# Attention with a mixture of experts on one core: routing in smaller pieces at two places of VectorE's step, the store of each slot tile right behind its copy, 79 slot tiles in place of 80

## The chip, the cores and the metric

One core of a Trainium2 chip runs the whole program. The metric is the device time of one execution in microseconds; less is better.

## The reference, cut to what matters

The input x has 16 sequences of 512 tokens with 256 features. Both branches read the same normalised rows.

```python
xn = layernorm(x)
# attention: 16 heads of 64, causal
q, k, v = xn @ Wq[h], xn @ Wk[h], xn @ Wv[h]
att = concat_h(softmax(causal(q @ k.T / 8)) @ v) @ Wo + bo
# mixture: 16 experts of width 128, the best two for each token
score = sigmoid(xn @ gate_w + gate_b)
value, index = top_k(score, 2);  value /= value.sum()
mlp(x, g, u, d) = (silu(x @ g) * (x @ u)) @ d
moe = xn + mlp(xn, shared) + sum_n value[n] * mlp(xn, expert[index[n]])
out = x + att + moe
```

## The kernel before, in words

**Stage A** (`stage_a`, about the first 100 us) normalises all rows, stores them to DRAM (`xn_rows`), splits the attention weights into a high and a low part for matmuls of three passes, and computes the gate scores.

**Stage D** (`stream`) runs over 128 units u, eight for each sequence; a unit is two heads of one sequence. One unit is a software pipeline: TensorE transposes the normalised probabilities of unit u (L685), computes the scores of unit u + 1 (L696), projects keys, values and queries of unit u + 2 (L658, L671), applies the output projection to a unit two back (L726), and at the end weighs the values of unit u (L710). VectorE takes the row maxima out of the score banks, splits keys and queries (L990) and attention outputs (L1001, the first instruction of its next step) and adds the output projection into `base` (L1015). ScalarE takes the exponentials (L853) and makes the high parts. GpSimd divides the probabilities (L1289) and issues the indirect DMAs. SyncE issues all other DMAs; its loop has four slots in each unit, and `pace` (L493) holds each slot until TensorE has come to a place of the unit: slot 0 waits for the first transposes, slot 1 for the last ones, slot 2 for the projected keys, slot 3 for the projected queries.

All TensorE results go through eight PSUM banks in ring order. `order` (L453) lists the bank users of a unit, and `emptied` (L464) says which semaphore frees a bank; TensorE waits for it before it writes. In a unit with slot tiles the last banks are taken by `dn`, `gu`, `xt` (a slot tile's output, its gate and up projection, its transposed rows) and `w`. So the first score banks of the next unit are the ones that the copy of `dn` (ScalarE, `take_y`, L893), the gate product of `gu` (VectorE, L1135 and L1140) and the split of `xt` (VectorE, `split_xt`, L1145) have to free, and the last of these four is freed by L1001. In a plain unit L1001 frees the same bank.

**The experts.** In units 0 to 9 VectorE runs one piece of `route(u)` (L1048) at the very end of each step: best two experts of each token, token counts by matmul with a matrix of ones (`count`, L757, at `SUMS_AT` and `RANKS_AT`), 16 prefix scans (L1075, L1078), a slot number for each token and expert, and the expert of each slot tile. The helper `then` puts a semaphore wait behind each routing instruction. Each expert's tokens fill whole slot tiles of 256 rows. From unit `FIRST_SCATTER` = 10 on, 32 units scatter the rows to their slots in DRAM (`queued_rows`), and every second unit from 12 on (`PACK_AT`) splits the weights of an expert on ScalarE and VectorE and stores them. `clear` (L513) has zeroed the slots before.

From `FIRST_TICK` = 46 on each unit has two ticks, part 0 after the scores and part 1 before L710. Tick n transposes tile n (L794), expands tile n - 1 (L784) and brings down tile n - 2 (L771). ScalarE copies the result of tile n - 2 into the one buffer `y` (L897), behind a wait for the store of the tile before it (`y_stored`). SyncE loads the rows two ticks ahead (L547) and stores `y` (`store_y`, L550). In the kernel before it stores tile n - 3 at tick n, in slot 1 for part 0 and slot 3 for part 1. GpSimd gathers each tile's weights (L1264).

After the last tick, from unit 88 on, `ITEMS` (L421) gives two blocks of 128 tokens to each unit: GpSimd gathers their two expert rows and VectorE adds them one unit later (`add_routed`, L1166). The last two sequences have their blocks in fixed units, 110 to 113 and 118 to 121, so that units 110 to 113 have three blocks each.

Of the kernel before, what the change touches and what calls it, by code (L numbers as in the profile page):

```python
# [25 lines left out]
ALU = mybir.AluOpType  # L26
# [3 lines left out]
P = 128  # L30
# [5 lines left out]
NTOK = B * T  # L36
# [9 lines left out]
SLOT_TILES = 2 * NTOK // SLOT_TILE + E  # L46
# [8 lines left out]
FIRST_SCATTER = 10  # L55
# [247 lines left out]
def stream(nc, ins, dram, keep, out):  # L303

    with ExitStack() as ctx:
# [65 lines left out]
        made, routing, both_ready, route_step = sem("made"), sem("routing"), sem("both_ready"), sem("route_step")  # L371
# [118 lines left out]
        with nc.Block() as block:  # L490
            @block.sync
            def _(sp):
# [96 lines left out]
                for u in STEPS:  # L589
                    b, k = u // PAIRS, u % PAIRS  # L590
                    for slot in range(4):
                        pace(u, slot)

                        if 0 <= u < ZERO_PARTS // 8:
                            for n in range(2):
                                clear(u * 8 + slot * 2 + n)
# [29 lines left out]
                        if n is not None and slot % 2:  # L626
# [341 lines left out]
            def _(dve):  # L968
# [79 lines left out]
                def route(u):  # L1048

                    if u == 0:  # L1050
# [4 lines left out]
                        mark_highest(0)  # L1055
                    elif u == 1:
                        choose(0)
                        then(dve.scalar_tensor_tensor(flat(gates), flat(chosen[0]), -4.0, flat(gates), ALU.mult, ALU.add))
                        then(dve.tensor_reduce(best[1][:, :], gates[:, :, :], AX.X, ALU.max))
                    elif u == 2:  # L1060
                        mark_ties(1)
                        choose(1)
                    elif u == 3:
# [5 lines left out]
                    elif u == SUMS_AT:  # L1069
# [4 lines left out]
                        for e in range(6):  # L1074
                            then(dve.tensor_tensor_scan(spots[:, :, e], ones[:, :], tile_sum[:, :, e], 0.0, ALU.mult, ALU.add))  # L1075
# [303 lines left out]
```

## Time and profile before

| what | value |
|---|---|
| median of 3 runs (lowest to highest) | 2058.46 us (2057.05 to 2064.8) |
| the profiled execution | 2058.73 us, its span 2057.0 us |
| mean granted TensorE clock over the span | 0.967 |
| TensorE busy | 1957.2 us, 95% |
| VectorE busy | 1406.4 us, 68% |
| ScalarE busy | 1204.1 us, 59% |
| GpSimd busy | 1015.5 us, 49% |
| chain that ended last | TensorE 70%, GpSimd 11%, issue 9% |

The busy share of TensorE is high, but a matmul that runs at half clock is busy too. So it is to be read together with the granted clock, and by stretches of the span and not over the whole. The span includes everything from the first instruction to the last; the execution's own time is 1.7 us above it.

### The profile page before, as it was taken

To read this page: it belongs to the slowest core of one execution; us is meant where nothing else is said; L and a number is where in the kernel's file an instruction comes from. 1 tells how busy PE (TensorE), PEld (TensorE's weight loads), DVE (VectorE), ACT (ScalarE), POOL (GpSimd) and SP (SyncE) were. 2 spreads that over 40 slices of the span, in tenths; PEclk is the share of its full clock that TensorE was granted. 3 is DMA by queue.
4 is the path that set the end of the run, shared out by engine and by line. 5 is a ranking of instruction groups with operands and counts; after the bars stand their busy time and mean duration, and the time that the engine had idled before them with its cause. 6 is when DMAs were issued, how large, how long until landed. Compare 5 with 4: busy or idle time off the path is not lost.

```text
span 2057.0 us, 53505 instructions
## 1 busy us (share of the span) xinstructions
PE 1957.2 (95%) x20580; PEld 1788.7 (87%) x20580; DVE 1406.4 (68%) x4090; ACT 1204.1 (59%) x3344; POOL 1015.5 (49%) x1513
## 2 busy tenths in 40 slices
PE   6889999999999999999999999999999999999998
PEld 6868888888898888898888898898898989888997
DVE  7567776767676756566566566566567888887775
ACT  4355556666665655556565565555566666655664
POOL 2232447777776543333333333343336777776552
PEclk9998999999999999999999999999999999998999
DMA  9524333434343224544544544444422232323100
GB/s 262 178 93 159 140 126 100 147 106 143 110 144 103 88 94 129 175 133 135 166 128 149 165 136 140 158 133 145 157 95 86 85 115 86 116 85 93 48 28 12
DMA packets 159435, 251.50 MB, mean 122 GB/s; under 512 B 27344, under 2 KB 113104, under 8 KB 159184
## 3 DMA queue, kind: packets, MB, share of 16 engines
q1 hardware_dynamic: 135376, 151.58, 22.8%
q0 software_dynamic: 23808, 96.49, 14.7%
q8 instruction: 167, 2.74, 0.6%
q14 instruction: 84, 0.69, 0.1%
HBM read 152.59 MB, written 95.42 MB: 121 GB/s over the span
## 4 chain that ended last, share of the span: by engine, by line
PE 70%; POOL 11%; issue 9%; DMA 2%; ACT 2%; DVE 1%; SPq 0%; POOLq 0%; ACTq 0%; DVEq 0%
PE d_bank L658 14%; PE d_bank L696 11%; PE d_bank L710 10%; PE d_bank L685 9%; PE d_bank L671 7%; POOL d_probs L1289 7%; PE d_bank L726 6%; PE d_bank L784 6%; POOL queued_rows L1252 4%; PE d_bank L771 3%; DMA routed_rows<-d_y 2%; PE d_bank L742 2%; PE d_bank L794 1%; ACT d_probs L853 1%; PE d_bank L731 1%
## 5 line engine op out<-in xcount | busy, mean ns | idle before, releaser
L1289 POOL TENSOR_SCALAR d_probs<-d_probs,d_inverse 128x512 f32<-128x512 f32 (+3 forms) x1024 | 550.6, 551 | 858.8 <-DVE d_inverse L985 857.1
L853 ACT ACTIVATE d_probs<-d_probs,d_bias 128x512 f32<-128x512 f32 (+3 forms) x1024 | 561.1, 553 | 1.2 <-DVE d_bias L979 1.2
L979 DVE CUSTOM_DVE_ANT_0 d_probs<-d_bank,mask 128x512 f32<-128x512 f32 (+3 forms) x1024 | 439.9, 484 | 5.1 <-PE d_bank L696 5.0
L658 PE MATMUL d_bank<-d_xnt,wqk_all 128*128 128x512 f32 x1536 | 422.7, 412 | 1.5 <-DVE d_xnt L1032 1.5
L696 PE MATMUL d_bank<-d_ks,d_qs 64*128 64x512 f32 (+3 forms) x3072 | 339.4, 348 | 53.7 <-issue 51.8
L696 PEld LDWEIGHTS d_bank<-d_ks,d_qs 64*128 64x128 f32 x3072 | 264.3, 197 | 85.3 <-issue 71.2
L658 PEld LDWEIGHTS d_bank<-d_xnt,wqk_all 128*128 128x128 f32 x1536 | 279.4, 194 | 56.7 <-DVE d_xnt L1032 1.7
L846 ACT ACTIVATE d_probs_t<-d_bank 128x512 f32<-128x512 f32 (+1 forms) x384 | 188.0, 525 | 234.0 <-PE d_bank L685 233.7
L710 PE MATMUL d_bank<-d_probs_t,d_v 128*64 128x128 f32 x5120 | 309.2, 276 | 0.0
L710 PEld LDWEIGHTS d_bank<-d_probs_t,d_v 128*64 128x64 f32 x5120 | 278.3, 137 | 17.1 <-issue 5.4
L685 PEld LDWEIGHTS d_bank<-ident_r,d_probs_moved 64*128 64x128 f32 x5120 | 237.7, 137 | 40.8 <-issue 38.3
L685 PE MATMUL d_bank<-ident_r,d_probs_moved 64*128 64x64 f32 x5120 | 260.6, 247 | 9.4 <-POOL d_probs L1289 9.3
L990 DVE TENSOR_TENSOR d_qs<-d_bank,d_qs 128x512 fp32r<-128x512 f32 x128 | 88.5, 692 | 199.6 <-ACT d_qs L859 199.6
L972 DVE COPY d_probs_t<-d_bank 128x512 f32<-128x512 f32 (+1 forms) x384 | 217.4, 594 | 4.6 <-PE d_bank L685 4.2
L671 PEld LDWEIGHTS d_bank<-wv_all,d_xnt 128*128 128x128 f32 x1536 | 202.9, 193 | 11.9
L726 PEld LDWEIGHTS d_bank<-wo_all,d_out_t 128*128 128x128 f32 x1536 | 200.1, 189 | 12.2 <-issue 1.7
L726 PE MATMUL d_bank<-wo_all,d_out_t 128*128 128x256 f32 x1536 | 205.8, 280 | 1.5 <-DVE d_out_t L1001 1.5
L871 ACT ACTIVATE d_out_t<-d_bank 128x512 fp32r<-128x512 f32 x128 | 76.0, 593 | 218.8 <-PE d_bank L710 215.8
L671 PE MATMUL d_bank<-wv_all,d_xnt 128*128 128x256 f32 x1536 | 203.6, 283 | 0.0
L853 ACT ACTIVATION_READ_ACCUMULATOR d_probs<-d_probs,d_bias 128x1 f32 x1024 | 196.2, 192 | 0.0
L1135 DVE SCALAR_TENSOR_TENSOR d_slot_hid<-d_slot_hid,d_bank 128x256 f32<-128x256 f32 x80 | 33.7, 421 | 211.8 <-ACT d_slot_hid L904 211.8
L897 ACT ACTIVATE d_y<-d_bank 128x512 f32<-128x512 f32 x80 | 47.8, 597 | 209.9 <-DMA routed_rows<-d_y 209.9
(124 smaller groups left out, 2473.5 us busy)
## 6 DMA issues: line engine op xcount, KB each, us to landing
queued_rows<-d_zeros SPq DMA_DIRECT2D x80, 256.0 KB, 2.4
d_x<-queued_rows SPq DMA_DIRECT2D x80, 256.0 KB, 3.1
routed_rows<-d_y SPq DMA_DIRECT2D x80, 256.0 KB, 3.8
expert_rows<-d_w SPq DMA_DIRECT2D x32, 384.0 KB, 3.0
a_x_in<-in_L_attn_x SPq DMA_DIRECT2D x16, 512.0 KB, 7.0
xn_rows<-a_xn SPq DMA_DIRECT2D x16, 512.0 KB, 5.2
d_normal<-xn_rows SPq DMA_DIRECT2D x32, 256.0 KB, 3.4
d_base<-in_L_attn_x SPq DMA_DIRECT2D x32, 256.0 KB, 3.1
```

The costliest lines, as they stand in the source:

```text
L658: last = pe.matmul(to[:, :], wqk[:, n % PAIRS, "qk".index(kind), wa, k, :], xnt[n // PAIRS % 2][:, xb, k, :], start=first, stop=(k == KD - ...
L671: last = pe.matmul(to[:, t * 2 * P:(t + 1) * 2 * P], xnt[b % 2][:, xa, k, tok * P:(tok + 1) * P], wv[:, wb, k, cols], start=(k == 0 and (x ...
L685: last = pe.transpose(to[r][:, off:off + DK].bitcast(F32R), moved[half(r), i, h, j * P:(j + 1) * P], ident[half(r), half(r)])
L696: last = pe.matmul(to[h][:, at * P:at * P + cols], qs[r][qa][half(h), i * P:(i + 1) * P], ks[r][kb][half(h), 0:cols], start=(n == 0), stop ...
L710: last = pe.matmul(to[half(h), i * P:(i + 1) * P], v[u // 2 % 2][:, j, col:col + DK], probs_t[fill][:, h, at + j, :], start=(j == 0), stop ...
L726: last = pe.matmul(to[:, s * D:(s + 1) * D], out_t[g % 2][oa][:, j, cols], wo[:, wb, g % 4 * GROUP + j, :], start=(j == 0 and n == 0), sto ...
L784: last = pe.matmul(to[:, part * SLOT_TILE:(part + 1) * SLOT_TILE], w[t % 3][:, wa, cols(k)], xt[:, xb, k, :], start=(n == 1), stop=(n == K ...
L846: act.activation(probs_t[fill][:, :, :, half(0)], bank(f"t{fill}", u)[:, 0:2 * slots * DK].rearrange("p (h j n) -> p h j n", h=2, n=DK), A ...
L853: act.activation(part, part, ACT.Exp, bias=bias[:, i, h:h + 1], scale=-1.0, accum_out=total[which][:, at % 4:at % 4 + 1]).then_inc(exp_don ...
L972: dve.tensor_copy(probs_t[fill][:, :, :, half(1)], bank(f"t{fill}", u, 1)[:, 0:2 * slots * DK].rearrange("p (h j n) -> p h j n", h=2, n=DK ...
L979: dve.tensor_tensor_reduce(out=probs[:, i, h, 0:cols], in0=bank(f"s{fill}", u, h)[:, at * P:at * P + cols], in1=mask[:, T - cols:T], scale ...
L1289: pool.tensor_scalar(part, part, inverse[which][:, at % 4:at % 4 + 1], 1.0, ALU.mult, ALU.mult).then_inc(norm_done, 1)
```

## The change

It has three parts. (1) `route` takes a second argument. Its early half runs after the maxima and the first `invert` of the step, ahead of the split of the keys; its late half runs where the whole piece ran. The work of units 0 to 9 is spread over units 0 to 12; the count matmuls move from units 4 and 6 to 5 and 8. `FIRST_SCATTER` goes from 10 to 12, the packs from even units from 12 on to odd units from 15 on, `FIRST_TICK` from 46 to 49. (2) `store_y(n - 2)` is issued in slot 2 of the unit for a tick of part 0, and in slot 0 of the next unit for a tick of part 1. (3) `SLOT_TILES` is 79 and not 80, and so is the number of `clear` transfers. The last tick is then part 0 of unit 89, the blocks of `ITEMS` begin in unit 91 and not in 88, and unit 118 has three of them too.

```diff
-SLOT_TILES = 2 * NTOK // SLOT_TILE + E
+SLOT_TILES = (2 * NTOK + E * (SLOT_TILE - 1)) // SLOT_TILE
-FIRST_SCATTER = 10
+FIRST_SCATTER = 12
...
-        PACK_AT = {FIRST_SCATTER + 2 + 2 * e: e for e in range(E)}
-        SUMS_AT, RANKS_AT = 4, 6
+        PACK_AT = {FIRST_SCATTER + 3 + 2 * e: e for e in range(E)}
+        SUMS_AT, RANKS_AT = 5, 8
-        FIRST_TICK = FIRST_SCATTER + 2 * B + 4
+        FIRST_TICK = FIRST_SCATTER + 2 * B + 5
...
-                        sp.wait_ge(routing, 9)
+                        sp.wait_ge(slots_known, 1)
...
-                        sp.wait_ge(routing, 10)
+                        sp.wait_ge(experts_known, 1)
...
-                            if 3 <= n:
-                                store_y(n - 3)
-                        if u == LAST_TICK + 1 and slot == 0:
-                            store_y(SLOT_TILES - 1)
+                        n = TICKS.get((u, 0)) if slot == 2 else TICKS.get((u - 1, 1)) if slot == 0 else None
+                        if n is not None and n >= 2:
+                            store_y(n - 2)
...
+                def mark_ties(n):
+                    then(dve.tensor_tensor(work[:, :, :], gates[:, :, :], by_e(best[n]), ALU.is_equal))
+                def rank_ties():
+                    then(dve.tensor_tensor(work[:, :, :], work[:, :, :], rank_of_e[:, None, :].broadcast_to([P, TT, E]),
+                                           ALU.mult))
+                def choose(n):
+                    then(dve.tensor_reduce(mark[:, :], work[:, :, :], AX.X, ALU.max))
+                    then(dve.tensor_tensor(chosen[n][:, :, :], work[:, :, :], by_e(mark), ALU.is_equal))
+                def scan(experts):
+                    for e in experts:
+                        then(dve.tensor_tensor_scan(spots[:, :, e], ones[:, :], tile_sum[:, :, e], 0.0, ALU.mult, ALU.add))
+                def spot_of(n):
+                    then(dve.tensor_tensor(work[:, :, :], chosen[n][:, :, :], spots[:, :, :], ALU.mult))
+                def slot_of(n):
+                    then(dve.tensor_reduce(mark[:, :], work[:, :, :], AX.X, ALU.add))
+                    then(dve.tensor_copy(keep["slot"][n][:, :], mark[:, :]))
+                def route(u, late):
+                    if (u, late) == (0, 0):
                         dve.wait_ge(made, 8)
                         then(dve.tensor_copy(rank_of_e[:, :], small["rank_i"][:, :]))
                         then(dve.tensor_copy(tile_start[:, :], tile_i[:, :]))
                         then(dve.tensor_copy(small["row"][:, 0:1], small["row_i"][:, 0:1]))
+                    elif (u, late) in ((0, 1), (2, 1)):
+                        n = u // 2
+                        then(dve.tensor_reduce(best[n][:, :], gates[:, :, :], AX.X, ALU.max))
+                        mark_ties(n)
+                    elif (u, late) in ((1, 0), (3, 0)):
+                        rank_ties()
+                    elif (u, late) in ((1, 1), (3, 1)):
+                        choose(u // 2)
+                    elif (u, late) == (2, 0):
                         then(dve.scalar_tensor_tensor(flat(gates), flat(chosen[0]), -4.0, flat(gates), ALU.mult, ALU.add))
+                    elif (u, late) == (4, 0):
                         then(dve.tensor_tensor(sum_best[:, :], best[0][:, :], best[1][:, :], ALU.add))
                         then(dve.reciprocal(sum_best[:, :], sum_best[:, :]))
                         for n in range(2):
                             then(dve.tensor_tensor(keep["weight"][n][:, :], best[n][:, :], sum_best[:, :], ALU.mult))
+                    elif (u, late) == (4, 1):
                         dve.tensor_tensor(both[:, :, :], chosen[0][:, :, :], chosen[1][:, :, :], ALU.add).then_inc(both_ready, 1)
+                    elif (u, late) == (SUMS_AT, 1):
                         dve.wait_ge(sums_ready, 1)
                         for n in range(2):
                             dve.tensor_copy(flat(tile_sum)[:, n * T:(n + 1) * T], bank(f"sum{n}", u)[:, :]).then_inc(sums_out, 1)
                         dve.wait_ge(sums_out, 2)
+                        scan(range(3))
+                    elif (u, late) == (6, 0):
+                        scan(range(3, 7))
+                    elif (u, late) == (6, 1):
+                        scan(range(7, E))
+                    elif (u, late) == (7, 0):
                         then(dve.tensor_scalar(padded[:, :], spots[:, TT - 1, :], float(SLOT_TILE - 1), None, ALU.add))
                         then(dve.tensor_copy(padded_i[:, :], padded[:, :]))
                         shift = SLOT_TILE.bit_length() - 1
...
                         then(dve.tensor_copy(padded[:, :], padded_i[:, :]))
                         then(dve.tensor_tensor_scan(ends[:, :], ones[:, 0:E], padded[:, :], 0.0, ALU.mult, ALU.add))
                         then(dve.tensor_tensor(offset[:, :], ends[:, :], padded[:, :], ALU.subtract))
+                    elif (u, late) == (7, 1):
                         then(dve.tensor_tensor(spots[:, :, :], spots[:, :, :], tile_sum[:, :, :], ALU.subtract))
                         then(dve.tensor_tensor(spots[:, :, :], spots[:, :, :], offset[:, None, :].broadcast_to([P, TT, E]),
                                                ALU.add))
+                    elif (u, late) == (RANKS_AT, 1):
                         dve.wait_ge(ranks_ready, 1)
                         for n in range(2):
                             part = flat(spots)[:, n * T:(n + 1) * T]
                             dve.tensor_tensor(part, bank(f"rank{n}", u)[:, :], part, ALU.add).then_inc(ranks_out, 1)
                         dve.wait_ge(ranks_out, 2)
+                    elif (u, late) in ((9, 0), (10, 0)):
+                        spot_of(u - 9)
+                    elif (u, late) in ((9, 1), (10, 1)):
+                        slot_of(u - 9)
+                        if u == 10:
+                            dve.sem_inc(slots_known, 1)
+                    elif (u, late) == (11, 1):
                         then(dve.tensor_tensor(past[:, :, :], tile_start[:, :, None].broadcast_to([P, SLOT_TILES, E]),
                                                ends[:, None, :].broadcast_to([P, SLOT_TILES, E]), ALU.is_ge))
+                    elif (u, late) == (12, 0):
                         then(dve.tensor_reduce(expert[:, :], past[:, :, :], AX.X, ALU.add))
+                    elif (u, late) == (12, 1):
                         then(dve.tensor_scalar(expert[:, :], expert[:, :], float(E - 1), float(P), ALU.min, ALU.mult))
                         then(dve.tensor_scalar(expert[:, :], expert[:, :], small["row"][:, 0:1], None, ALU.add))
                         then(dve.tensor_copy(keep["weight_row"][:, :], expert[:, :]))
+                        dve.sem_inc(experts_known, 1)
...
                         invert(31, u + 1)
+                    route(u, 0)
...
-                    if 0 <= u < 10:
-                        route(u)
+                    route(u, 1)
```

`mark_ties` is one comparison, `rank_ties` one multiplication, `choose` a reduction and a comparison, `spot_of` one multiplication, `slot_of` a reduction and a small copy; `scan` is one prefix scan for each expert.

## Rows read from the trace of the kernel before

**Rows 1.** By stretch: length, busy PE, PEld, DVE, ACT, POOL, then clock, DMA share, GB/s.

```profile
128.00:302.00 174.00, 157.67 (x1586) 138.44 (x1586) 130.98 (x346) 89.67 (x255) 66.32 (x107) 0.89 0.40 138
...
738.00:1529.00 791.00, 757.27 (x7664) 701.11 (x7660) 489.71 (x1390) 461.59 (x1263) 283.55 (x448) 0.95 0.45 143
1529.00:1832.00 303.00, 302.48 (x3454) 273.52 (x3452) 242.17 (x714) 190.25 (x553) 213.86 (x304) 1.00 0.31 95
1832.00:1894.00 62.00, 58.52 (x590) 51.09 (x589) 47.50 (x130) 32.73 (x94) 47.57 (x63) 0.89 0.32 95
```

**Rows 2.** Waits of the slot stage, 738 to 1529 us: total us, times, longest.

```profile
ACT d_y L897 <- DMA routed_rows<-d_y: 209.9, 78, 7.6
...
PE d_bank L696 <- issue: 31.2, 32, 3.7
```

**Rows 3.** Timeline around one stall: start us, us, engine, line, what, idle before it.

```profile
974.73 1.63 PE L658 MATMUL d_bank<-d_xnt,wqk_all 128*128 128x512 f32 x6
...
977.26 1.08 POOL L1264 DMA_INDIRECT d_w<-expert_rows,weight_row  x1 [0.17 <-issue]
...
980.42 0.87 PE L771 MATMUL d_bank<-d_w,d_slot_hs 128*128 128x256 f32 x6
...
980.69 0.71 SPq L552 DMA_DIRECT2D routed_rows<-d_y  x1
...
987.85 0.60 ACT L897 ACTIVATE d_y<-d_bank 128x512 f32<-128x512 f32 x1 [7.32 <-DMA routed_rows<-d_y]
...
989.55 0.68 DVE L1145 TENSOR_TENSOR d_xt<-d_bank,d_xt 128x512 fp32r<-128x512 f32 x1
...
989.74 2.67 PE L696 MATMUL d_bank<-d_ks,d_qs 64*128 64x512 f32 x12 [3.28 <-issue]
```

**Rows 4.** Stores of y, line L552, from issue to landing.

```profile
DMA to landing us min/median/max: 2.1/3.8/7.6
```

**Rows 5.** As rows 1: eight plain units, one slot unit, a gap and what followed.

```profile
379.40:481.20 101.80, 100.46 (x1156) 91.36 (x1154) 71.72 (x213) 66.40 (x188) 72.86 (x105) 1.00 0.38 126
...
1010.70:1028.30 17.60, 17.60 (x192) 16.61 (x192) 9.56 (x31) 10.60 (x30) 6.27 (x10) 1.00 0.45 144
...
1102.80:1106.20 3.40, 2.07 (x32) 1.57 (x31) 2.57 (x6) 2.88 (x7) 0.00 (x0) 1.00 0.55 221
1106.20:1124.40 18.20, 18.20 (x168) 16.68 (x168) 12.38 (x34) 10.62 (x29) 7.72 (x12) 1.00 0.40 120
```

**Rows 6.** Chain of waits, 1062 to 1084 us: start us, us, what.

```profile
1065.36 0.64 issue
...
1066.95 0.71 issue
...
1072.84 2.22 PE d_bank L784 x12
...
1081.74 1.44 PE d_bank L784 x12
```

**Rows 7.** Timeline of TensorE at the first slot tile.

```profile
743.51 0.72 PE L794 MATMUL d_bank<-ident_r,d_x 128*128 128x128 f32 x4 [2.45 <-DVE d_bias L979]
```

**Rows 8.** Timeline of VectorE and TensorE in unit 2 and behind it.

```profile
163.06 0.69 DVE L990 TENSOR_TENSOR d_qs<-d_bank,d_qs 128x512 fp32r<-128x512 f32 x1 [2.34 <-ACT d_qs L859]
...
164.53 1.22 DVE L1116 TENSOR_TENSOR d_work<-gates,d_best 128x1024 f32<-128x1024 f32 x1
...
169.85 0.69 DVE L1001 TENSOR_TENSOR d_out_t<-d_bank,d_out_t 128x512 fp32r<-128x512 f32 x1
...
170.64 1.01 PE L696 MATMUL d_bank<-d_ks,d_qs 64*128 64x256 f32 x6 [2.60 <-issue]
```

**Rows 9.** The same in unit 9 and behind it.

```profile
271.95 1.49 DVE L1102 TENSOR_TENSOR d_past<-d_tile_start,d_ends 128x1280 f32<-128x1280 f32 x1
...
276.67 1.01 PE L696 MATMUL d_bank<-d_ks,d_qs 64*128 64x256 f32 x6 [2.52 <-issue]
```

**Rows 10.** Timeline of VectorE, unit 4: six scans.

```profile
197.51 1.93 DVE L1075 TENSOR_TENSOR_SCAN d_spots<-d_ones,d_tile_sum 128x64 f32<-128x64 f32 x6
```

More of the change, by code:

```diff
@@ L370, in stream @@
         zeroed, zero_stored = sem("zeroed"), sem("zero_stored")
-        made, routing, both_ready, route_step = sem("made"), sem("routing"), sem("both_ready"), sem("route_step")
+        made, both_ready, route_step = sem("made"), sem("both_ready"), sem("route_step")
+        slots_known, experts_known = sem("slots_known"), sem("experts_known")
         sums_ready, sums_out, ranks_ready, ranks_out = sem("sums_ready"), sem("sums_out"), sem("ranks_ready"), sem("ranks_out")
@@ L592, in _ @@
                         pace(u, slot)
-                        if 0 <= u < ZERO_PARTS // 8:
-                            for n in range(2):
-                                clear(u * 8 + slot * 2 + n)
+                        for n in range(u * 8 + slot * 2, u * 8 + slot * 2 + 2):
+                            if 0 <= n < ZERO_PARTS:
+                                clear(n)
                         if u in (FIRST_SCATTER - 1, FIRST_SCATTER):
@@ L1073, in route @@
                         dve.wait_ge(sums_out, 2)
-                        for e in range(6):
-                            then(dve.tensor_tensor_scan(spots[:, :, e], ones[:, :], tile_sum[:, :, e], 0.0, ALU.mult, ALU.add))
-                    elif u == 5:
-                        for e in range(6, E):
-                            then(dve.tensor_tensor_scan(spots[:, :, e], ones[:, :], tile_sum[:, :, e], 0.0, ALU.mult, ALU.add))
+                        scan(range(3))
[4 more added lines that the diff above has]
+                    elif (u, late) == (7, 0):
                         then(dve.tensor_scalar(padded[:, :], spots[:, TT - 1, :], float(SLOT_TILE - 1), None, ALU.add))
@@ L1086, in route @@
                         then(dve.tensor_tensor(offset[:, :], ends[:, :], padded[:, :], ALU.subtract))
-                    elif u == RANKS_AT:
+                    elif (u, late) == (7, 1):
                         then(dve.tensor_tensor(spots[:, :, :], spots[:, :, :], tile_sum[:, :, :], ALU.subtract))
@@ L1095, in route @@
                         dve.wait_ge(ranks_out, 2)
-                    elif u in (7, 8):
-                        n = u - 7
-                        then(dve.tensor_tensor(work[:, :, :], chosen[n][:, :, :], spots[:, :, :], ALU.mult))
-                        then(dve.tensor_reduce(mark[:, :], work[:, :, :], AX.X, ALU.add))
-                        then(dve.tensor_copy(keep["slot"][n][:, :], mark[:, :]))
-                    elif u == 9:
+                    elif (u, late) in ((9, 0), (10, 0)):
[5 more added lines that the diff above has]
+                    elif (u, late) == (11, 1):
                         then(dve.tensor_tensor(past[:, :, :], tile_start[:, :, None].broadcast_to([P, SLOT_TILES, E]),
                                                ends[:, None, :].broadcast_to([P, SLOT_TILES, E]), ALU.is_ge))
+                    elif (u, late) == (12, 0):
                         then(dve.tensor_reduce(expert[:, :], past[:, :, :], AX.X, ALU.add))
+                    elif (u, late) == (12, 1):
                         then(dve.tensor_scalar(expert[:, :], expert[:, :], float(E - 1), float(P), ALU.min, ALU.mult))
@@ L1107, in route @@
                         then(dve.tensor_copy(keep["weight_row"][:, :], expert[:, :]))
-                    dve.sem_inc(routing, 1)
-                def mark_highest(n):
-                    then(dve.tensor_reduce(best[n][:, :], gates[:, :, :], AX.X, ALU.max))
-                    mark_ties(n)
-                def mark_ties(n):
-                    then(dve.tensor_tensor(work[:, :, :], gates[:, :, :], by_e(best[n]), ALU.is_equal))
-                    then(dve.tensor_tensor(work[:, :, :], work[:, :, :], rank_of_e[:, None, :].broadcast_to([P, TT, E]),
-                                           ALU.mult))
-                def choose(n):
-                    then(dve.tensor_reduce(mark[:, :], work[:, :, :], AX.X, ALU.max))
-                    then(dve.tensor_tensor(chosen[n][:, :, :], work[:, :, :], by_e(mark), ALU.is_equal))
+                        dve.sem_inc(experts_known, 1)
                 def split_hidden(u):
```

11 lines of the change are left out of this document (removed).

## The prediction

> **What bounds the kernel now.** I read the windows by stretch first, then the waits of the worst stretch, then its timeline. In the windows the reader compares three columns: the length, the busy time of TensorE, and its granted clock. In the plain units from 1529 to 1832 us TensorE is idle for 0.5 of 303 us at clock 1.00: these are at their floor. In the slot stage, 738 to 1529 us, it is idle for 791.0 - 757.3 = 33.7 us, and the clock of 0.95 costs 0.05 * 791 = 40 us more. The first units (128 to 302 us) have 16.3 us idle and 0.11 * 174 = 19 us of clock; 1832 to 1894 us has 3.5 and 0.11 * 62 = 7 us [rows 1]. TensorE bounds all of it, and what can be won is its idle time and the half clock behind it.
>
> In the slot stage ScalarE waits 209.9 us, 78 times, for the store of `y` to land, and TensorE 31.2 us in front of L696 for something the view can't name ("issue") [rows 2]. The timeline names it: a store is issued at 980.69, ScalarE's next copy starts only at 987.85 when it has landed, VectorE's split of `xt` follows at 989.55, and TensorE's scores stand 3.28 us until 989.74, because they write the banks that these instructions free [rows 3]. The copy had long been done when its store was issued, since the store has its place half a unit behind it; so landing times of 2.1, 3.8 (median) and 7.6 us [rows 4] fall just in front of the next copy.
>
> How the clock hangs on this: the two small gaps at 1065.36 and 1066.95 us are followed by expansions of 2.22 us in place of 1.44 [rows 6]: 1.2 instead of 2.4 GHz. After 1.3 us of gap at 1102.8 to 1106.2 the clock stayed 1.00 [rows 5]. So a gap makes a fall likely, not certain; where there is none (1529 to 1832 us) there is no fall.
>
> **Part 2, the store.** For a tick of part 0 the store is now issued once the keys are projected. In the unit of rows 3 L658 ends at 974.73 + 1.63 = 976.4, and ScalarE makes that tick's copy ahead of its split of those keys: the store starts some 4 us earlier than 980.69, and is ahead of the weight gather at 977.26. With 3.8 us it lands at 980.2, before the next result is due (980.42 + 0.87 = 981.3); with 7.6 us at 984.0. TensorE stands only if the copy comes later than about 984.5: the copy at 987.85 cost 3.28 us. For part 1 it is issued behind the first transposes of the next unit; the next copy is due some 5 to 7 us behind them (in the unit of rows 6 the expansion L784 that follows its matmuls starts at 1072.84, 7.5 us behind the transposes). There 3.8 us fit, and 7.6 us make a wait of up to 2 us on ScalarE with no TensorE work soon behind it. So nearly all of the idle time goes. What stays is the start: the first tile's rows are loaded in the very unit that transposes them, 2.45 us [rows 7], plus a fall, together some 4 us; and I leave 3 us for the units in which `base`, `normal` and `partial` are moved in slots 2 and 3 ahead of the store on SyncE. Gain 33.7 + 40 - 4 - 3 = 67; the undisturbed units say a little less: one takes 17.6 us against 101.8 / 8 = 12.7 in a plain one, 4.9 for two tiles [rows 5], which over 41 units (the first and last partly filled) leaves some 65 us of excess, 61 without the start. I take 60, after the 3 us. Bounds: 30 (the clock falls stay) and 70. The new wait on SyncE (for the copy) has in its queue behind it the loads of rows for the next tick, which are due half a unit later; it costs nothing unless a copy is over 4 us late. What is late next is nothing: ScalarE is busy 461.6 and VectorE 489.7 of 791 us [rows 1].
>
> **Part 1, the routing.** Today a piece ends the step and L1001 waits behind it. In unit 2 four instructions of 1.2 to 1.4 us run from 164.53 to 169.85, 5.3 us, and TensorE stands 2.60 us: some 2.7 us fit [rows 8]. In unit 9 the shared expert fills the end of the step; a piece of 3.9 us (271.95 to about 275.9) costs 2.52 us, so 1.4 fit [rows 9]. New late pieces: two instructions of 1.25, 2.5 us, in units 0 to 3; at most nine scans in unit 6, at 1.93 / 6 = 0.32 [rows 10] 2.9 us; two instructions of 2.7 in unit 7; 1.3 to 2.3 elsewhere. With 1.4 us of room in units 0 and 1 (1.1 us over in each), about 1.9 in unit 3 (0.6), 2.7 in units 6 and 7 (0.2 each) and 0.5 for units 8 to 12, the gaps sum to 3.7 in place of 16.3. The early pieces, 0.5 to 1.5 us, lie in the 2.34 us that VectorE waits for the queries [rows 8]; they delay the split of the keys, which no one needs before the next unit, so zero; if that cover were gone, 13 units by 1.2 would be 15 us. The clock: with three gaps of near 1 us I keep about 7 of 19 us. Gain 12.6 + 12 = 24 to 25; bounds 10 (cover half gone, falls stay) and 33. The packs move to odd units, where VectorE has 0.6 us more of its own and the same room as above for their one instruction; zero, bounds 0 and 6. Scatters, packs and ticks keep their spacing and only start later.
>
> **Part 3, one tile less.** A tile is 4.9 / 2 = 2.4 us of TensorE [rows 5]; one transfer of `clear` less is hidden behind other work.
>
> **The end.** A unit with three blocks costs: units 110 to 113 hold 10 us of idle time and clock in three stalled units [rows 1], 3.4 each. Unit 118 becomes another one, so plus 3. All others keep two blocks.
>
> Sum, against the profiled execution of 2058.7 (span 2057.0 and 1.7 around it), which stands within 0.3 of the median: 2058.7 - 60 - 24.5 - 2.4 + 3 = 1974.8. I say **1975**.
>
> **The clock rule.** By the trace, gaps as small as 0.64 and 0.71 us precede falls [rows 6]. The Trainium skill, page "TensorE: Matmul & The Clock Gate", section "HAM oscillation — how this bites in real kernels", tells of falls only after idle stretches longer than any gap but one or two here. If that were all, these falls would have another cause and would survive: only idle time would go. That is rival A.
>
> **Rivals.**
> A. The falls stay in the slot stage and in the routing units. Then 33.7 - 7 = 27, 12.6, 2.4 are won and 3 lost: 2020. For it: after like gaps the clock fell once and once it did not [rows 5, 6], so another cause may have its part. Against: none in 303 us of plain units, and fall follows gap in rows 6. Chance 0.12.
> B. Part of the stores still land late. SP reaches slot 2 behind up to three other transfers in two units of eight, and the store now runs beside the gather. If a third of the gaps and falls stay, 24 us less is won, with somewhat more left in the routing: 2000. Chance 0.22.
> C. The other side: the stores collide with the gathers of weights. At 45% DMA share [rows 1] a store takes the longest time seen, 7.6 us. Then part 1's copy slips 2 to 3 us into each unit, ScalarE passes that on to the query split, and TensorE stands perhaps 1.2 us and loses 1.7 by clock in each of 40 units: 116 us in place of 74 today, 42 more, against 24.5 + 2.4 - 3 won: 2077. It decides from a landing of over 6 us in most units. The Trainium skill, page "DMA: Bandwidth & Descriptors", section "Issuing engines are not separate DMA queues", says that transfers of SyncE and GpSimd share the same engines and interleave, which is this collision's ground. Against: the median is 3.8 with loads and gathers under way already. Chance 0.03.
> D. The stalls at L696 come from elsewhere and the store only shifts a wait: parts 1 and 3 alone, 2058.7 - 24.5 - 2.4 + 3 = 2035; if the routing then also gains nothing, 2058. Chance 0.06, of which 0.02 within 0.5% of today.
>
> **Numbers.** My forecast (1960 to 1990) has 0.57. The range holds forecast and B and most of the spread between: 1958 to 2008; A, C and D lie outside. A measurement of this kernel tells 0.5% (10 us) from no change. Faster by over that: 0.95; within: 0.02; slower: 0.03.
>
> **What would show it.** ScalarE's wait for the store falls from 209.9 us to under 40; the waits in front of L696 in the slot stage to under 6 us; the clock of that stretch at 0.99 or more; eight slot units take about 142 us. In units 1 to 13 the idle time is near 4 us and at most two falls remain; a gap of about 1.4 us appears behind unit 119. Wrong would be: a clock that stays near 0.95 without gaps (A), copies that still wait 3 us (B), landings of 6 us and more (C), or gaps of the same size with no ScalarE wait (D).

## The result and the profile after

| | before | after |
|---|---|---|
| median of the runs of the result | 2058.70 us (4 runs) | 1968.07 us (4 runs, 1964.47 to 1973.94) |
| profiled execution, its span | 2058.73 us, 2057.0 us | 1970.11 us, 1968.4 us |
| mean granted TensorE clock over the span | 0.967 | 0.989 |

The ratio is 0.9557, 95% interval 0.9525 to 0.9589: 91 us less, where 84 were forecast and 1958 to 2008 us was the range. The page of the profile after: busy time, the span in 40 slices, the granted clock in tenths.

```profile
PE 1905.5 (97%) x20558; PEld 1751.7 (89%) x20558; DVE 1406.9 (71%) x4086; ACT 1208.4 (61%) x3340; POOL 1019.5 (52%) x1512
...
PE   6889999999999998999999999999999999999998
...
PEclk9999999999999999999999999999999999999999
```

TensorE's busy time fell by 51.7 us with almost the same instructions. Only one tile of work (some 2.4 us) is saved. TensorE runs at half clock for 138 us before and for 47 us after, and half of that difference, 46 us, is busy time that went. Such a stretch at 1.2 GHz is called a fall from here on. The windows, by stretch (length; busy PE, PEld, DVE, ACT, POOL; clock, DMA share, GB/s), answer to [rows 1]. The bounds are, within 0.5 us, the ends of L710 in units 0, 16, 48, 89, 109 and 127; the last row is eight undisturbed units of the slot stage.

```profile
131.20:342.90 211.70, 207.33 (x2300) 185.22 (x2299) 172.54 (x473) 128.23 (x370) 103.62 (x161) 0.98 0.36 127
...
752.30:1478.00 725.70, 718.78 (x7654) 674.45 (x7650) 488.62 (x1390) 467.00 (x1261) 286.23 (x452) 0.99 0.48 155
1478.00:1730.00 252.00, 251.65 (x2892) 228.08 (x2890) 202.06 (x594) 158.73 (x461) 175.24 (x249) 1.00 0.31 96
1730.00:1960.00 230.00, 221.45 (x2500) 199.30 (x2498) 173.13 (x500) 134.95 (x391) 143.64 (x208) 0.97 0.22 66
863.20:1003.40 140.20, 140.20 (x1508) 131.86 (x1506) 95.87 (x273) 92.08 (x248) 56.34 (x88) 1.00 0.50 163
```

In the slot stage (752.3 to 1478.0 us) TensorE is idle for 6.9 us and the clock is 0.99; before it was 33.7 us and 0.95. Eight undisturbed units take 140.2 us at clock 1.00 and without a microsecond of idle time.

Read off both traces by the same ends of units, and the half clock added up in each stretch:

| stretch | before, us (at half clock) | after, us (at half clock) |
|---|---|---|
| to the end of unit 0 | 128.0 (0) | 130.9 (3.4) |
| units 1 to 16 | 236.2 (37.5) | 211.7 (10.2) |
| plain units to the first tick, and from the last tick to unit 109 (52 units) | 664.6 (3.4) | 661.3 (3.4) |
| slot stage, 41 units | 791.1 (78.5) | 725.8 (13.7) |
| units 110 to 127 | 228.3 (17.1) | 229.8 (13.7) |

The stage of 41 units now begins and ends with a unit that holds the shared expert, and before with a shorter kind; so it has 3.3 us of length from the plain stretches, and its own gain is 791.1 - 725.8 + 3.3 = 68.6 us. The waits of the stage (total us, times, longest) answer to [rows 2]:

```profile
ACT d_y L897 <- PE d_bank L771: 55.1, 34, 2.9
...
ACT d_y L897 <- DMA routed_rows<-d_y: 6.3, 4, 5.4
...
PE d_bank L794 <- DMA d_x<-queued_rows: 4.6, 1, 4.6
...
PE d_bank L696 <- issue: 1.8, 2, 1.1
```

ScalarE's wait for the store went from 209.9 us and 78 times to 6.3 us and 4 times. TensorE's waits in front of L696 went from 31.2 us to 1.8. One typical store, in the view of [rows 3]:

```profile
905.00 0.36 SPq L553 DMA_DIRECT2D routed_rows<-d_y  x1
...
907.46 1.09 POOL L1280 DMA_INDIRECT d_w<-expert_rows,weight_row  x1 [0.16 <-issue]
...
911.80 0.87 PE L771 MATMUL d_bank<-d_w,d_slot_hs 128*128 128x256 f32 x6
...
912.71 0.60 ACT L897 ACTIVATE d_y<-d_bank 128x512 f32<-128x512 f32 x1 [2.93 <-PE d_bank L771]
...
915.36 0.68 DVE L1161 TENSOR_TENSOR d_xt<-d_bank,d_xt 128x512 fp32r<-128x512 f32 x1
...
917.67 1.32 PE L696 MATMUL d_bank<-d_ks,d_qs 64*128 64x512 f32 x12
```

The store is issued at 905.00, ahead of the weight gather; ScalarE reaches the next copy, is held up only by TensorE's own result of 911.80 to 912.67, and starts it at 912.71. The split of `xt` (now L1161) is done 1.6 us before TensorE asks for its bank at 917.67, and the scores run without a gap. Stores also land sooner, against [rows 4]:

```profile
DMA to landing us min/median/max: 2.1/2.3/8.3
```

### The profile page after: what moved, and what is told of

Same layout as the page of the kernel before. It is cut to its first block, busy times and chain, and to the rows that moved or that the text cites. A ratio compares the mean times of both kernels' runs of the same rounds, so it can differ in the third digit from the quotient of the medians.

```text
span 1968.4 us, 53517 instructions
## 1 busy us (share of the span) xinstructions
PE 1905.5 (97%) x20558; PEld 1751.7 (89%) x20558; DVE 1406.9 (71%) x4086; ACT 1208.4 (61%) x3340; POOL 1019.5 (52%) x1512
## 4 chain that ended last, share of the span: by engine, by line
PE 73%; POOL 12%; issue 7%; ACT 2%; DVE 1%; DMA 0%; POOLq 0%; SPq 0%; DVEq 0%
PE d_bank L658 15%; PE d_bank L710 11%; PE d_bank L696 10%; PE d_bank L685 9%; PE d_bank L671 7%; POOL d_probs L1305 7%; PE d_bank L726 7%; PE d_bank L784 6%; POOL queued_rows L1268 4%; PE d_bank L771 3%; PE d_bank L742 2%; ACT d_probs L853 2%; PE d_bank L794 1%; PE d_bank L731 1%; POOL d_base L1257 1%
## 5 line engine op out<-in xcount | busy, mean ns | idle before, releaser
L658 PE MATMUL d_bank<-d_xnt,wqk_all 128*128 128x512 f32 x1536 | 417.6, 408 | 1.5 <-DVE d_xnt L1032 1.5
L696 PE MATMUL d_bank<-d_ks,d_qs 64*128 64x512 f32 (+3 forms) x3072 | 317.4, 335 | 14.0 <-issue 12.0
L710 PE MATMUL d_bank<-d_probs_t,d_v 128*64 128x128 f32 x5120 | 308.6, 276 | 0.0
L710 PEld LDWEIGHTS d_bank<-d_probs_t,d_v 128*64 128x64 f32 x5120 | 277.7, 137 | 17.2 <-issue 5.4
L696 PEld LDWEIGHTS d_bank<-d_ks,d_qs 64*128 64x128 f32 x3072 | 252.0, 188 | 35.6 <-issue 19.4
L685 PEld LDWEIGHTS d_bank<-ident_r,d_probs_moved 64*128 64x128 f32 x5120 | 232.8, 136 | 38.6 <-issue 36.9
L685 PE MATMUL d_bank<-ident_r,d_probs_moved 64*128 64x64 f32 x5120 | 256.2, 244 | 10.1 <-POOL d_probs L1305 10.0
L1001 DVE TENSOR_TENSOR d_out_t<-d_bank,d_out_t 128x512 fp32r<-128x512 f32 x128 | 88.3, 690 | 113.5 <-ACT d_out_t L871 112.8
L1296 POOL DMA_INDIRECT d_rows<-routed_rows,slot x128 | 132.0, 1031 | 35.5 <-issue 33.6
```

The lines of the kernel that those rows point to most:

```text
L658: last = pe.matmul(to[:, :], wqk[:, n % PAIRS, "qk".index(kind), wa, k, :], xnt[n // PAIRS % 2][:, xb, k, :], start=first, stop=(k == KD - ...
L685: last = pe.transpose(to[r][:, off:off + DK].bitcast(F32R), moved[half(r), i, h, j * P:(j + 1) * P], ident[half(r), half(r)])
L696: last = pe.matmul(to[h][:, at * P:at * P + cols], qs[r][qa][half(h), i * P:(i + 1) * P], ks[r][kb][half(h), 0:cols], start=(n == 0), stop ...
L710: last = pe.matmul(to[half(h), i * P:(i + 1) * P], v[u // 2 % 2][:, j, col:col + DK], probs_t[fill][:, h, at + j, :], start=(j == 0), stop ...
L1296: pool.indirect_dma_start(out=rows[m % 4 // 2][:, m % 2 * 2 + n, :], out_offset=None, in_=dram["routed"][:, :], in_offset=bass.IndirectOff ...
```

## The experiments

Two theories were put against each other first. The one of the prediction: the late store of `y` holds the PSUM banks that the next unit's scores need, and each such gap can bring TensorE down from 2.4 to 1.2 GHz for some microseconds. The rivals: the clock falls have another cause (A), or the stalls come from elsewhere (D). In each group of runs the kernel before ran on the same chip; it had medians of 2059.5, 2060.4 and 2057.8 us.

**The old places of the store.**

```diff
-                        n = TICKS.get((u, 0)) if slot == 2 else TICKS.get((u - 1, 1)) if slot == 0 else None
-                        if n is not None and n >= 2:
-                            store_y(n - 2)
+                            if 3 <= n:
+                                store_y(n - 3)
+                        if u == LAST_TICK + 1 and slot == 0:
+                            store_y(SLOT_TILES - 1)
```

> The changed kernel with the stores of y back at their old places (tick n stores tile n - 3, in slot 1 and slot 3, behind the load of the next rows); routing and 79 tiles stay as changed. My theory (the late store holds the banks that TensorE's scores need, and the clock falls follow those gaps): about 2035 us, the slot stage again with some 30 us of idle time and a clock near 0.95, ScalarE waiting some 200 us for the store. Rival (the routing's gain carries most): under 2000 us. Rival D (the stalls come from elsewhere): 1968 us as before.

Measured: 2042.32 us, ratio to before 0.9916 (0.9892 to 0.9939). ScalarE waits 196.8 us for the store again, and the window over the 41 units of the stage shows the old length and the old clock:

```profile
754.80:1545.90 791.10, 759.52 (x7654) 702.11 (x7652) 489.94 (x1390) 461.39 (x1261) 284.89 (x452) 0.95 0.44 142
```

The whole stage is back, 791.1 us, with nothing else undone. 74 us hang on these lines.

**The store alone**, in the kernel before.

```diff
-                            if 3 <= n:
-                                store_y(n - 3)
-                        if u == LAST_TICK + 1 and slot == 0:
-                            store_y(SLOT_TILES - 1)
+                        n = TICKS.get((u, 0)) if slot == 2 else TICKS.get((u - 1, 1)) if slot == 0 else None
+                        if n is not None and n >= 2:
+                            store_y(n - 2)
```

> The kernel before with only the new places of the stores of y (tile n - 2, slot 2 and slot 0 of the next unit); routing at one place, 80 tiles. My theory: 2058.7 - 66 = about 1993 us; the slot stage without gaps and at clock 0.99 or more, units 1 to 10 as before with 16 us of gaps and clock 0.89. If the parts overlap, this run and the one with the old store place would not add up: their gains would sum to clearly more or less than the 90 us of the whole.

Measured: 1986.90 us, ratio 0.9637 (0.9616 to 0.9658), 73 us less than before. The windows over the slot stage and over units 1 to 16:

```profile
742.10:1464.60 722.50, 718.79 (x7662) 675.16 (x7662) 487.47 (x1390) 468.20 (x1263) 285.59 (x450) 0.99 0.48 157
131.20:368.80 237.60, 220.78 (x2300) 196.35 (x2300) 173.15 (x475) 130.36 (x372) 109.78 (x169) 0.91 0.37 128
```

The stage takes 722.5 us with 80 tiles, and the first units stay as they were (237.6 us, clock 0.91). The gains add up within the noise: 73 us of the store here and 17 of the rest in the run with the old store make 90, and the whole is 91. So no overlap of the parts shows.

**Only one of the two places early.**

```diff
-                        n = TICKS.get((u, 0)) if slot == 2 else TICKS.get((u - 1, 1)) if slot == 0 else None
+                        n = TICKS.get((u, 0)) if slot == 2 else TICKS.get((u - 1, 1)) if slot == 1 else None
```

> The changed kernel, but only the stores of part-0 ticks are early (slot 2); those of part-1 ticks are issued in slot 1 of the next unit, behind the row loads. My theory: only the copy near the end of a unit stands in front of the next unit's scores, and it waits for the part-0 store; so this one loses almost nothing, 1968 to 1975 us, with ScalarE waiting about 1 us for the store at each part-0 copy. Rival (ScalarE's lost time itself is the cost, wherever it falls): 40 waits of 1 us and more, 1990 us or above.

Measured: 1967.54 us, ratio 0.9553 (0.9531 to 0.9574): nothing lost. ScalarE's wait in the slot stage is real all the same:

```profile
ACT d_y L897 <- DMA routed_rows<-d_y: 37.2, 38, 3.0
```

There is no wait in front of L696 among the waits of this stage. 37 us of ScalarE's time, 1.0 us for each copy that waits and 3.0 at the most, cost nothing.

```diff
-                        n = TICKS.get((u, 0)) if slot == 2 else TICKS.get((u - 1, 1)) if slot == 0 else None
+                        n = TICKS.get((u, 0)) if slot == 3 else TICKS.get((u - 1, 1)) if slot == 0 else None
```

> The changed kernel, but only the stores of part-1 ticks are early (slot 0 of the next unit); those of part-0 ticks are issued in slot 3, behind the row loads. My theory: this is where the whole cost lay, so 2020 to 2035 us, gaps in front of L696 in the slot stage and a clock near 0.95. Rival (both places share the cost): near 2000 us.

Measured: 2039.72 us, ratio 0.9929 (0.9897 to 0.9961), a little above what was expected. Of the stage's waits:

```profile
ACT d_y L897 <- DMA routed_rows<-d_y: 172.4, 39, 7.9
...
PE d_bank L696 <- issue: 31.1, 35, 3.6
```

Half as many copies wait as in the kernel before, yet the loss is the whole one. These copies, the last of each unit, wait for the part-0 store, and the banks that TensorE wants next stand behind them. They are also the ones with the long waits: 4.4 us each (172.4 / 39) against 1.0 us (37.2 / 38) at the other place, and at this place too some twenty waits, up to 4.6 us, have no gap behind them. No run has long waits at the other place; so whether such waits would cost something there was not tried. One slot of SyncE's loop for the part-0 store, which also puts it ahead of the load of rows, is worth over 70 us (2039.72 against 1967.54).

**79 tiles alone**, in the kernel before.

```diff
-SLOT_TILES = 2 * NTOK // SLOT_TILE + E
+SLOT_TILES = (2 * NTOK + E * (SLOT_TILE - 1)) // SLOT_TILE
...
-                        if 0 <= u < ZERO_PARTS // 8:
-                            for n in range(2):
-                                clear(u * 8 + slot * 2 + n)
+                        for n in range(u * 8 + slot * 2, u * 8 + slot * 2 + 2):
+                            if 0 <= n < ZERO_PARTS:
+                                clear(n)
```

> The kernel before with 79 slot tiles and 79 clears only. My theory: one tile is 2.4 us of TensorE plus its share of the stage's stalls, 1 us: 2055 us, not to be told from 2058.7. Rival (the last tile's end matters more, since the gathers of the end wait for it): 2050 us or below.

Measured: 2057.75 against 2060.41 us, ratio 0.9983 (0.9968 to 0.9999): 2.7 us, about what a tile was reckoned at (2.4), at the edge of what 10 and 13 runs can tell from nothing.

**Gaps made on purpose**, in plain units that had none in front of the scores.

```diff
                     route(u, 1)
+                    if u in range(18, 38, 2):
+                        for _ in range(3):
+                            then(dve.tensor_reduce(mark[:, :], wqk[:, 0, :, :, :, :].bitcast(F32).rearrange(
+                                "p w a k (c e) -> p (w a k c) e", e=E), AX.X, ALU.max))
```

> The changed kernel with three more reductions of 1.22 us each at the end of VectorE's step in ten plain units (18, 20 to 36), where the trace showed no gap in front of the scores and no fall of the clock. It adds only work whose result nobody reads. My theory (a gap in front of the scores makes the clock fall): a gap of 1.0 to 1.3 us behind each of the ten, 11 us in all, and several falls of the granted clock right behind them, each 1.7 to 3.4 us more: 20 to 35 us over the changed kernel. Rival A (the falls have another cause, tied to the slot tiles): the ten gaps, 11 us, and the clock of that stretch stays 1.00.

Measured: 1996.26 us in its one execution, 28 us over the changed kernel. The timeline behind unit 22, the third of the ten, and then windows up to that gap, right behind it, and over the stretch with the added reductions:

```profile
422.24 3.72 DVE L1249 TENSOR_REDUCE d_mark<-wqk_all 128x64 f32<-128x1024 f32 x3
...
426.00 0.69 DVE L1001 TENSOR_TENSOR d_out_t<-d_bank,d_out_t 128x512 fp32r<-128x512 f32 x1
...
426.79 0.62 PE L696 MATMUL d_bank<-d_ks,d_qs 64*128 64x256 f32 x6 [1.34 <-issue]
```

```profile
342.30:427.00 84.70, 80.49 (x927) 72.11 (x925) 66.39 (x172) 51.88 (x145) 57.87 (x83) 1.00 0.37 123
427.80:434.60 6.80, 6.80 (x38) 6.10 (x36) 4.57 (x19) 4.60 (x14) 3.65 (x6) 0.50 0.41 136
342.30:611.10 268.80, 256.63 (x2796) 229.27 (x2794) 206.84 (x539) 161.91 (x452) 180.48 (x254) 0.96 0.36 118
```

Three reductions keep L1001 until 426.00, TensorE stands 1.34 us, and 1 us later its clock is 0.50 for 6.8 us. All ten units show a gap, of 1.03 to 1.43 us, 12.8 us together; six of the ten are followed by a fall within 2.5 us. Units 17 to 48 hold 37.5 us at half clock in place of 3.4; 3.4 us of the growth belong to a fall that the changed kernel has too, behind a gap of 2 us in front of L685, and that lasts longer here. TensorE's idle time in these units grew from 6.1 to 16.2 us, since some shorter waits went. 10.1 + 34.1 / 2 = 27.2 us is the growth of that stretch (438.1 against 409.3 us, 28.8 us) to 2 us. No slot tile is at work in these units, and a gap alone brings falls: rival A's other cause isn't needed. The two gaps before this one (1.4 and 1.0 us) brought no fall, so a gap of this size makes one likely and not certain. All this rests on one execution.

**The second place of the routing taken away**, its spread over 13 units kept.

```diff
                         invert(31, u + 1)
-                    route(u, 0)
...
+                    route(u, 0)
                     route(u, 1)
```

> The changed kernel, but the early halves of the routing run at the end of the step too, directly ahead of the late halves; the spread over units 0 to 12 stays. My theory: some 13 us of early pieces come behind the late ones in units that have 1.4 to 2.7 us of room, so about 8 us of gaps more and 5 to 8 us of clock: 1980 to 1985 us, all of it in units 1 to 13. Rival (spreading over 13 units was the gain and the second place adds nothing): 1968 to 1970 us.

Measured: 1988.73 us, against 1962.27 for the change in the same group of runs; ratio to before 0.9640 (0.9602 to 0.9679). The window over units 1 to 16:

```profile
130.80:367.30 236.50, 223.52 (x2300) 198.87 (x2300) 171.74 (x473) 128.87 (x369) 98.18 (x162) 0.90 0.32 113
```

236.5 us: to 0.3 us the length in the kernel before. Seven gaps of 1.1 to 2.4 us, 11.8 us together, stand in place of four, and 47.8 us run at half clock in place of 10.2. I had expected 1980 to 1985 us, and it is more, because more falls followed. Against the kernel before, the spreading alone saved 4.7 us of idle time here and had 10.3 us more at half clock; the run with the store alone has the same ratio (0.9637). So the spreading alone shows no gain, and the routing's 24.5 us come with the place ahead of the key split (whether the place would do it without the spreading was not tried).

**The change again, in the last group.**

> The changed kernel once more, on the same chip as the three others: 1966 to 1970 us by any theory. It shows whether the late store of the first profile comes again: my theory says it is rare, so the slot stage without that gap, 719 to 721 us over 41 units.

Measured: 1962.27 us, ratio 0.9526 (0.9499 to 0.9553), a little below what I expected. Its slot stage takes 718.8 us; the late store of the first profile (told of below) is missing. But it isn't rare, as I had written: of the seven profiles with this order of the stores, that of this run alone is without the gap behind unit 66.

**Four mends of what was left.** Blocks of the end spread; first rows loaded a unit earlier; the store first in its slot; fewer scans in one piece.

```diff
-            for _ in range(2):
+            for _ in range(2 - sum(u == item[0] for item in ITEMS)):
                 if waiting and u >= waiting[0][0] * PAIRS + 12:
```

> The changed kernel, but a unit that holds a fixed block of the last two sequences takes only one waiting block, so that no unit has three. My theory: the five gaps of 0.6 to 2 us behind units 111 to 114 and 119, 6.5 us in all, go with their falls of the clock (10 us at half clock, 5 us): 1957 to 1960 us. Rival (the gaps come from the gathers' landing or from SyncE, not from VectorE's third block): no change, 1968 us.

Measured: 1955.23 us, ratio 0.9490 (0.9465 to 0.9515). The window from 1730 to 1850 us, in which the changed kernel had 5.0 us of idle time:

```profile
1730.00:1850.00 120.00, 119.83 (x1349) 107.95 (x1347) 97.36 (x290) 77.17 (x226) 88.34 (x125) 1.00 0.30 91
```

All five gaps are gone, and units 110 to 127 take 218.8 us in place of 229.8.

```diff
                         if n is not None and slot % 2:
-                            if n == 0:
-                                load_slots(0)
...
+                        if u == FIRST_TICK - 1 and slot == 3:
+                            load_slots(0)
```

> The changed kernel, but the rows of slot tile 0 are loaded in slot 3 of the unit before the first tick. My theory: the 4.6 us that TensorE stands in front of the first slot transposes and the 6.8 us at half clock behind it go, 1960 to 1962 us. Rival (something else of the first tick is late next, such as the gathered weights): under 2 us of it.

Measured: 1961.95 us, ratio 0.9523 (0.9500 to 0.9545). The wait in front of the first L794 is gone: the first unit of the stage takes 17.5 us, in place of 24.6 and 22.5 in the two profiles of the change. Its median stands 6 us under one run of the change and level with the other, and neither was in its group; so the 5 to 7 us are shown by the unit, not by the medians.

The third mend puts the three lines with `store_y(n - 2)` ahead of `store_attended` in the slot, on top of the two others:

> The changed kernel with the blocks spread and the first rows early as in the two runs before, and the store of y issued first in its slot, ahead of the transfers of base, normal and partial. My theory: the gains of 13 and 6 us add up, and the third edit only removes the rare late store (at most 6 us in the one execution that had it): 1948 to 1952 us. Rival (ahead of the others the store delays the normal rows and something new is late): above 1955 us.

Measured: 1948.84 us, ratio 0.9456 (0.9428 to 0.9484). The slot stage has no fall at all, takes 713.5 us (its window, by the ends of L710), and the gap behind unit 66 is missing, here and in the next run:

```profile
754.50:1468.00 713.50, 712.94 (x7654) 669.37 (x7652) 488.19 (x1390) 466.64 (x1260) 286.20 (x452) 1.00 0.48 158
```

```diff
-                        scan(range(7, E))
+                        scan(range(7, 13))
                     elif (u, late) == (7, 0):
+                        scan(range(13, E))
+                    elif (u, late) == (7, 1):
...
-                    elif (u, late) == (7, 1):
                         then(dve.tensor_tensor(spots[:, :, :], spots[:, :, :], tile_sum[:, :, :], ALU.subtract))
+                    elif (u, late) == (8, 0):
                         then(dve.tensor_tensor(spots[:, :, :], spots[:, :, :], offset[:, None, :].broadcast_to([P, TT, E]),
```

> The same as the three mends, with the scans as 3, 4, 6 and 3 over units 5 to 7, so that the nine at the end of unit 6 become six, and the additions behind them in units 7 and 8. My theory: the gap of 1.0 us behind unit 6 and its fall go, 2 to 4 us under the three mends. Rival (the gap moves to the end of unit 7 or 8): no change.

Measured: 1945.86 us, ratio 0.9446 (0.9420 to 0.9473), the fastest version, but its interval and that of the three mends overlap. The profile takes the rival's side: the gap behind unit 6 (1.00 us) is gone and one of 0.83 us stands behind unit 7. Units 1 to 16 take 212.1 us and took 211.5. Its profile is 2.3 us shorter than that of the three mends, and the end of unit 0, which the scans can't touch, comes 3.4 us earlier. So the 3 us are not shown to be the scans' doing.

## Why the prediction was right

**The store (60 us, with the tile 62).** The step that named the stall was right: TensorE's "issue" waits in front of L696 were the banks of `dn`, `gu` and `xt`, held up by the late landing. The size was too small: 68.6 us in the profiled execution, 73 in the runs with the store alone. Of two counts I took the lower one, and it was worked out wrong. Idle time and clock gave 33.7 + 40 us; the undisturbed unit gave "some 65". But 791 - 41 x 17.6 is 69, and more with the first and last unit partly filled; 65 goes only with the 142 us for eight units that the prediction names later. Eight undisturbed ones take 140.2 us: three take 17.6, four 16.9 and the one with the shared expert 19.7. The count by idle time and clock fell short too. It has 33.7 + 39.3 us before and 6.9 + 6.8 after, 59 us of gain and 62 with the tile, against 68.6. The missing 7 us lie in what the profile calls busy: by the trace the scores of L696, at equal clock, take 6.6 us less in the stage with the store alone than before. Without a gap a matmul of them adds about 0.1 us to the busy time, since it overlaps the one ahead; the 32 right behind a gap add 0.45 us each (8 of them at half clock). So a gap costs somewhat more than its idle time. What the prediction kept back for late stores, 3 us, came at a single place, unit 66, where `partial` and `normal` rows are moved ahead of the store. A store and a gather are issued there in the same instant, and the store lands 8.3 us later:

```profile
1065.69 1.88 SPq L553 DMA_DIRECT2D routed_rows<-d_y  x1
1065.70 1.08 POOL L1280 DMA_INDIRECT d_w<-expert_rows,weight_row  x1 [0.16 <-issue]
...
1074.08 0.60 ACT L897 ACTIVATE d_y<-d_bank 128x512 f32<-128x512 f32 x1 [5.40 <-DMA routed_rows<-d_y]
...
1075.96 0.96 PE L696 MATMUL d_bank<-d_ks,d_qs 64*128 64x512 f32 x6 [1.06 <-issue]
```

Those two gaps, 1.1 + 0.7 us, and their fall are 5 of the 7 us between this stage and that of the run of the change in the last group. So rival B's mechanism exists, at one of the five units with these transfers and not at a third of all; why at this one stays open. With the store first in its slot it was seen in neither of two profiles. Rival C did not come: stores land in 2.3 us at the median, at a DMA share of 0.48.

**The start of the slot stage (4 us left).** It was more. TensorE waits 4.6 us (above, L794) and not the 2.45 of [rows 7], and a fall of 6.8 us sets in before the wait is over. The first unit of the stage takes 24.6 us, and 17.5 with the first rows loaded early: 7 us where 4 were kept.

**The routing (24.5 us).** Units 1 to 16 went from 236.2 to 211.7 us, 24.5. The room at the end of a step was read rightly. Behind unit 1 (1.1 us foreseen) and unit 6 (0.2 foreseen):

```profile
144.90 1.21 DVE L1056 TENSOR_REDUCE d_mark<-d_work 128x64 f32<-128x1024 f32 x1
...
147.40 0.69 DVE L1001 TENSOR_TENSOR d_out_t<-d_bank,d_out_t 128x512 fp32r<-128x512 f32 x1
...
148.19 0.62 PE L696 MATMUL d_bank<-d_ks,d_qs 64*128 64x256 f32 x6 [1.19 <-issue]
```

```profile
211.87 3.29 DVE L1061 TENSOR_TENSOR_SCAN d_spots<-d_ones,d_tile_sum 128x64 f32<-128x64 f32 x9
...
215.19 0.69 DVE L1001 TENSOR_TENSOR d_out_t<-d_bank,d_out_t 128x512 fp32r<-128x512 f32 x1
...
215.98 0.62 PE L696 MATMUL d_bank<-d_ks,d_qs 64*128 64x256 f32 x6 [1.00 <-issue]
```

The gaps behind units 0, 1, 3 and 6 are 0.6, 1.2, 0.6 and 1.0 us, 3.4 in all for 3.7 foreseen. That the sum fits so well is partly luck: unit 0 came out at half of what was foreseen, and unit 6 at 1.0 us for 0.2. There nine scans took 3.3 us and not 2.9, and some 2.3 us fit and not 2.7. That the early halves cost nothing holds too: no other gap stands in front of L696 in these units. The half clock left, 10.2 us, costs 5 us where 7 were kept.

**One tile (2.4 us).** 2.7 us in the medians of the run with 79 tiles alone.

**The end (3 us more).** The new unit with three blocks has its gap, 1.5 us for 1.4 foreseen, and a fall of 6.8 us:

```profile
1864.84 0.68 DVE L1001 TENSOR_TENSOR d_out_t<-d_bank,d_out_t 128x512 fp32r<-128x512 f32 x1
...
1865.62 0.84 PE L696 MATMUL d_bank<-d_ks,d_qs 64*128 64x256 f32 x6 [1.52 <-issue]
```

The stretch as a whole grew by 1.5 us only, by luck with the falls: the gaps behind units 111 to 114 brought one of 3.4 us this time and three of 13.7 us together before. Unit 0 ended 2.9 us later, 1.7 of them from a fall. With the old routing it ends at 128.0, 128.6 and 131.2 us in three profiles, with the new one at 129.0 to 133.0 in eleven; whether the change has a part in that stays open.

**The clock.** The section "HAM oscillation — how this bites in real kernels" of the Trainium skill's page "TensorE: Matmul & The Clock Gate", named in the prediction, tells of falls after long idle stretches. Here the made gaps of 1.0 to 1.4 us brought falls six times in ten, so the measurement decides against taking long stretches as the only ones.

The sum came out at 1975 for 1968: the store's term, with the tile, was too small by 6 us in the profiled execution and by 13 in the medians, and the 3 us too little for the start are already in that. In the profile the end was better by 1.5 us than foreseen, and unit 0 worse by 2.9.

## What to carry to other kernels

Look for the copy that ends last in front of a bank that TensorE wants, and give its releaser (here a store) the first place behind its producer in its queue; shorter waits elsewhere may cost nothing. Price a short TensorE gap at itself plus the half clock behind it: here the clock was 46 of the 89 us that the profiled span lost. Work put into an engine's step belongs where that engine already waits, and not at the end of the step, where the next unit's release stands behind it.

## What the runs showed of the hardware that was not expected

Gaps in TensorE's work of 1.03 to 1.43 us, in a kernel that is otherwise dense, were followed by a fall from 2.4 to 1.2 GHz in six of ten cases. Each fall lasted 3.4 or 6.8 us, 30.7 us together, so a gap of 1.3 us cost 1.3 + 1.5 us on average.

Stores of the same 256 KB landed in 3.8 us (median) when all were issued right behind a load of 256 KB, and in 2.3 us when all were issued ahead of it. With the part-0 stores alone ahead it was 3.1 us, with the part-1 stores alone 3.7. The part-0 store gained most: its median went from 4.6 to 2.1 us. So the earlier place won time twice, in the issue and in the flight. The distance of the store from the gather of the weights changed as well, and no run tells load and gather apart.
